# A fused embedding, attention and mixture-of-experts kernel: 16-bit turns, half-block turning moved, stores moved, last rows gathered elsewhere

## The reference

```python
h = tok(x)                                  # weight[x] + lora, times magnitude and a column norm
# attention: 16 heads of 32, every projection on quantised activations and weights
def act_quant(x):
    scale = 127 / clip(max(abs(x), -1), 1e-5)
    return clip(round(x * scale), -128, 127) / scale
bitlinear = lambda x, w: act_quant(x) @ weight_quant(w).T      # ternary weights
h = h + bitlinear(softmax(q k^T / sqrt(32)) v, w_o)            # q, k, v = bitlinear(layernorm(h), w)
# experts: a shared one of 704, and 2 of 8 routed ones of 352
g = softmax(x Wr^T); top 2
h = h + (silu(x Wsg^T) * (x Wsu^T)) Wsd + sum over the 2 of g_e * ((silu(x Wg_e^T) * (x Wu_e^T)) Wd_e)
```

## Time and profile before

| | us |
|---|---|
| median of 3 runs | 1512.48 |
| lowest, highest | 1511.66, 1517.18 |
| profiled execution | 1511.87 |
| its span in the trace | 1509.7 |

### The profile page before, as it was taken

One profiled execution on the slowest core, in us unless ns is written; L12 is line 12 of the kernel. 1 busy time (PEld: TensorE's weight loads), 2 busy tenths in 40 slices (PEclk: granted clock), 3 DMA queues, 4 the chain that ended last, 5 costly groups with the idle time before them and its releaser, 6 DMA issues.

```text
span 1509.7 us, 37446 instructions
## 1 busy us (share of the span) xinstructions
PE 1403.1 (93%) x14294; PEld 1146.5 (76%) x14294; DVE 1117.8 (74%) x2215; ACT 875.3 (58%) x1502; POOL 393.2 (26%) x494
## 2 busy tenths in 40 slices
PE   6587869999999996899999999999999999999997
PEld 1122147777777774899999998989889898999996
DVE  4477848889889885776647777877778777677776
ACT  4688936777777774433325666656556665533331
POOL 6500054444444420003211211111111110133333
PEclk9899979999999997899999999999999999999999
DMA  9999942223223111131114678777787776543365
GB/s 342 392 378 362 418 129 58 66 64 84 63 64 82 56 47 54 56 116 56 42 43 142 233 255 272 239 262 249 255 275 235 274 240 236 188 140 131 125 241 177
DMA packets 77905, 269.42 MB, mean 178 GB/s; under 512 B 9696, under 2 KB 10336, under 8 KB 71392
## 3 DMA queue, kind: packets, MB, share of 16 engines
q1 hardware_dynamic: 61360, 223.88, 41.0%
q0 software_dynamic: 16432, 44.05, 11.1%
HBM read 224.12 MB, written 43.78 MB: 177 GB/s over the span
## 4 chain that ended last, share of the span: by engine, by line
PE 33%; DVE 10%; issue 7%; ACT 7%; DMA 3%; POOL 0%; SPq 0%; ACTq 0%; POOLq 0%; DVEq 0%
PE up_ps L1734 6%; PE up_ps L1736 6%; PE up_ps L1735 6%; PE down_ps L1735 4%; PE down_ps L1736 4%; PE down_ps L1734 4%; DVE w_split L1509 3%; ACT w_split L1424 3%; DMA slot_rows<-y_rows 2%; DVE xT_lo L1500 2%; PE up_ps L1768 1%; DVE h L1645 1%; PE up_ps L1763 1%; DVE w_split L1510 1%; ACT h_hi L1446 1%
## 5 line engine op out<-in xcount | busy, mean ns | idle before, releaser
L1734 PE MATMUL up_ps<-xT_hi,w_split 128*128 128x256 f32 x1280 | 366.4, 286 | 15.6 <-DVE xT_lo L1500 8.3
L1736 PE MATMUL up_ps<-xT_hi,w_split 128*128 128x256 f32 x1280 | 362.8, 283 | 0.0
L1735 PE MATMUL up_ps<-xT_lo,w_split 128*128 128x256 f32 x1280 | 362.8, 283 | 0.0
L1734 PEld LDWEIGHTS up_ps<-xT_hi,w_split 128*128 128x128 f32 x1280 | 245.6, 192 | 18.6 <-issue 8.6
L1735 PEld LDWEIGHTS up_ps<-xT_lo,w_split 128*128 128x128 f32 x1280 | 245.7, 192 | 1.3
L1736 PEld LDWEIGHTS up_ps<-xT_hi,w_split 128*128 128x128 f32 x1280 | 245.6, 192 | 0.0
L1446 ACT ACTIVATE h_hi<-h 128x256 fp32r<-128x256 f32 (+1 forms) x192 | 80.2, 418 | 264.8 <-DVE h L1645 202.3
L1397 POOL DMA_INDIRECT xr<-x_rows,slot_tokens x71 | 71.5, 1006 | 426.1 <-PE xT_ps L1829 381.6
L1424 ACT ACTIVATE w_split<-w_stage 128x1408 fp32r<-128x1408 f32 (+1 forms) x123 | 169.1, 1411 | 4.4 <-PE down_ps L1736 1.8
L1734 PE MATMUL down_ps<-w_split,h_hi 128*128 128x512 f32 (+1 forms) x405 | 159.1, 393 | 1.4 <-DVE H L1629 1.4
L1736 PE MATMUL down_ps<-w_split,h_lo 128*128 128x512 f32 (+1 forms) x405 | 160.2, 396 | 0.0
(11 more groups left out here) (301 smaller groups left out, 3000.3 us busy)
## 6 DMA issues: line engine op xcount, KB each, us to landing
W<-table SPq DMA_DIRECT2D x48, 1280.0 KB, 8.7
w_stage<-packed SPq DMA_DIRECT2D x80, 704.0 KB
w_stage<-packed SPq DMA_DIRECT2D x40, 768.0 KB
xr<-x_turned SPq DMA_DIRECT2D x32, 512.0 KB
slot_rows<-y_rows SPq DMA_DIRECT2D x32, 512.0 KB
x_rows<-x SPq DMA_DIRECT2D x32, 256.0 KB, 2.0
x_turned<-x2T SPq DMA_DIRECT2D x32, 256.0 KB, 3.8
out<-H SPq DMA_DIRECT2D x32, 256.0 KB
```

Of the source, the lines that this page charges most:

```text
L1734: pe.matmul(out, a_hi, b_hi, start=first, stop=False)
L1735: pe.matmul(out, a_hi, b_lo, start=False, stop=False)
L1736: return pe.matmul(out, a_lo, b_hi, start=False, stop=last)
```

## The change

Four edits, as the diff has them. First, z and z2 are made with `ROUNDER + LOW_HALF`, LOW_HALF being 2^14, so that the low 16 bits of each f32 hold 16384 plus the integer. PE transposes only these 16-bit words, as bf16 with stride two and with the bf16 identity, into the first half of bank[3], and ACT reads them as int16, minus LOW_HALF. Second, the half block's h is turned into `route_ps`, after the first up part of the next block, and the wait for h_lo before up_ps[2] is gone. Third, SP issues the store of y ahead of the third weight piece. Fourth, the rows of the last two sequences are gathered into `xr[0]` and `xr[1]`, once the last block's rows have been read from them; sequences 28 to 31 are combined within the last block's body, 28 ahead of its last gate, and the last block's result is added to H last; SP's last four stores wait for that too.

```diff
...
 ROUNDER = 1.5 * 2.0**23
+LOW_HALF = 2.0**14
...
         bank = [ps(f"bank{i}", [P, 512]) for i in range(4)]
+        turned_words = bank[3][:, :].bitcast(mybir.dt.int16)[:, 0:D].rearrange("p (k t) -> p k t", k=KT)
...
                     act.wait_ge(quant2_done, back1.next)
-                    act.activation(z2[:, :], attn[:, :], ACT.Copy, bias=ROUNDER, scale=quant2[:, 0:1]).then_inc(z2_done, 1)
+                    act.activation(z2[:, :], attn[:, :], ACT.Copy, bias=ROUNDER + LOW_HALF, scale=quant2[:, 0:1]).then_inc(z2_done, 1)
...
                     act.wait_ge(aq_turned, back1.next)
-                    act.activation(aqT[:, :, :], bank[3][:, :].rearrange("p (k t) -> p k t", k=KT), ACT.Copy, bias=-ROUNDER).then_inc(aqT_done, 1)
+                    act.activation(aqT[:, :, :], turned_words, ACT.Copy, bias=-LOW_HALF).then_inc(aqT_done, 1)
...
                     after(act, xq_turned, ahead2.i - 1)
-                    act.activation(z[ahead2.b][:, :], y[ahead2.b][:, :], ACT.Copy, bias=ROUNDER, scale=quant[ahead2.b][:, 0:1]).then_inc(z_done, 1)
+                    act.activation(z[ahead2.b][:, :], y[ahead2.b][:, :], ACT.Copy, bias=ROUNDER + LOW_HALF, scale=quant[ahead2.b][:, 0:1]).then_inc(z_done, 1)
...
                     act.wait_ge(xq_turned, ahead2.next)
-                    act.activation(xqT[ahead2.b][:, :, :], bank[3][:, :].rearrange("p (k t) -> p k t", k=KT), ACT.Copy, bias=-ROUNDER).then_inc(xqT_done, 1)
+                    act.activation(xqT[ahead2.b][:, :, :], turned_words, ACT.Copy, bias=-LOW_HALF).then_inc(xqT_done, 1)
...
                 return mm
+            def turn_words(tile):
+                words = tile[:, :].bitcast(BF16)[:, 0::2]
+                for k in range(KT):
+                    mm = pe.transpose(bank[3][:, :].bitcast(BF16)[:, k * T:(k + 1) * T], words[:, k * P:(k + 1) * P], ident_b[:, :])
+                return mm
...
                         pe.wait_ge(xqT_done, now.next)
-                    turn(bank[3], z[ahead1.b]).then_inc(xq_turned, 1)
+                    turn_words(z[ahead1.b]).then_inc(xq_turned, 1)
...
                         pe.wait_ge(aqT_done, back2.next)
-                    turn(bank[3], z2).then_inc(aq_turned, 1)
+                    turn_words(z2).then_inc(aq_turned, 1)
...
             return 2 * no if ROUTED[r] == "B" else FULL_BLOCKS + no
+        def routed_tiles(odd):
+            return sum(2 if ROUTED[r] == "B" else 1 for r in range(odd, ROUTED_BLOCKS, 2))
...
             return "A" if n < B_FROM else ROUTED[n - B_FROM] if n < C_FROM else "C"
...
         def _(sp):
-            def load_weights(w, expert):
+            def load_weights(w, expert, before_last=None):
                 for piece, (a, b) in enumerate(PIECES):
+                    if piece == 2 and before_last is not None:
+                        store_rows(before_last)
...
                 sp.dma_start(xr[odd][:, :, :], x2T_dram[bass.ds((n - first) * 2, 2), :, :].rearrange("s p d -> p s d")).then_inc(rows_in[odd], 16)
-            def block_weights(r):
-                load_weights(r + 1, sp.value_load(block_expert[0:1, bass.ds(plan_no(r), 1)], min_val=0, max_val=EXPERTS - 1))
+            def block_weights(r, before_last=None):
+                load_weights(r + 1, sp.value_load(block_expert[0:1, bass.ds(plan_no(r), 1)], min_val=0, max_val=EXPERTS - 1), before_last)
...
             for r in range(ROUTED_BLOCKS - 3):
-                block_weights(r + 3)
-                store_rows(r)
+                block_weights(r + 3, r)
             load_rows(C_FROM, C_FROM % 2, C_FROM)
-            load_weights(LAST_W, EXPERTS + 1)
-            store_rows(ROUTED_BLOCKS - 3)
+            load_weights(LAST_W, EXPERTS + 1, ROUTED_BLOCKS - 3)
...
                 sp.dma_start(out[bass.ds(i, 1), :, :].rearrange("s p d -> (s p) d"), row(H, i)).then_inc(out_stored, 16)
-            with sp.Fori(0, SEQS) as i:
+            with sp.Fori(0, SEQS - 4) as i:
+                store_out(i)
+            for i in range(SEQS - 4, SEQS):
+                sp.wait_ge(y_taken, 2 * N - SEQS + i + 1)
...
             for i in range(SEQS):
-                after(pool, combined, (i - 1) * TOP)
+                if i < SEQS - 2:
+                    after(pool, combined, (i - 1) * TOP)
+                    rows, arrived = comb[i % 2], comb_in
+                else:
+                    pool.wait_ge(xT_lo_done, N)
+                    rows, arrived = xr[i % 2], rows_gathered
                 for t in range(TOP):
-                    pool.indirect_dma_start(out=comb[i % 2][:, t, :], out_offset=None, in_=y_dram,
-                                            in_offset=bass.IndirectOffsetOnAxis(ap=slot_i[:, t * SEQS + i:t * SEQS + i + 1], axis=0)).then_inc(comb_in[i % 2], 16)
+                    pool.indirect_dma_start(out=rows[:, t, :], out_offset=None, in_=y_dram,
+                                            in_offset=bass.IndirectOffsetOnAxis(ap=slot_i[:, t * SEQS + i:t * SEQS + i + 1], axis=0)).then_inc(arrived[i % 2], 16)
...
                 after(act, down_done, (n - 1) * 2)
-                act.activation(h_hi[odd][:, 0:2, 0:P], up_ps[2][:, 0:2 * P].rearrange("p (j t) -> p j t", j=2), ACT.Copy).then_inc(h_hi_done, 2)
-                act.activation(h_hi[odd][0:96, 2, 0:P], up_ps[2][0:96, 2 * P:3 * P], ACT.Copy).then_inc(h_hi_done, 1)
+                act.activation(h_hi[odd][:, 0:2, 0:P], route_ps[:, 0:2 * P].rearrange("p (j t) -> p j t", j=2), ACT.Copy).then_inc(h_hi_done, 2)
+                act.activation(h_hi[odd][0:96, 2, 0:P], route_ps[0:96, 2 * P:3 * P], ACT.Copy).then_inc(h_hi_done, 1)
...
                         dve.tensor_tensor(row(H, i), row(H, i), down_ps[r][:, :], ALU.add).then_inc(y_taken, 1)
-            def combine(i, odd):
-                dve.wait_ge(comb_in[odd], (i - odd) * TOP * 8 + TOP * 16)
+            def combine(i, odd, rows):
+                if rows is comb[odd]:
+                    dve.wait_ge(comb_in[odd], (i - odd) * TOP * 8 + TOP * 16)
+                else:
+                    dve.wait_ge(rows_gathered[odd], 16 * (TOP + routed_tiles(odd)))
...
                         dve.wait_ge(combined, i * TOP + t)
-                    dve.scalar_tensor_tensor(out=row(H, i), in0=comb[odd][:, t, :], scalar=gate_values[:, bass.ds(i, 1), t],
+                    dve.scalar_tensor_tensor(out=row(H, i), in0=rows[:, t, :], scalar=gate_values[:, bass.ds(i, 1), t],
                                              in1=row(H, i), op0=ALU.mult, op1=ALU.add).then_inc(combined, 1)
-            def gate_full(n, odd):
+            def gate_full(n, odd, before_last=None):
                 for j, (_, f) in enumerate(F_TILES):
+                    if before_last and j == 2:
+                        before_last()
...
                 for count, at, rows in ((2, 0, P), (3, 2, 96)):
-                    turned_h = up_ps[2][0:rows, at * P:count * P].rearrange("p (j t) -> p j t", j=count - at)
+                    turned_h = route_ps[0:rows, at * P:count * P].rearrange("p (j t) -> p j t", j=count - at)
...
                     gate_half_rows(n)
+                elif kind_after:
+                    gate_full(n, odd)
                 else:
-                    gate_full(n, odd)
+                    gate_full(n, odd, lambda: combine(SEQS - 4, 0, comb[0]))
+                    dve.wait_ge(combined, (SEQS - 3) * TOP)
...
                     dve.wait_ge(y_taken, n * 2)
-                    if not isinstance(n, int) or n > C_FROM + 1:
+                    if kind_after:
                         for r in range(2):
-                            combine((n - (C_FROM + 1)) * 2 + r, r)
+                            combine((n - (C_FROM + 1)) * 2 + r, r, comb[r])
+                    else:
+                        combine(SEQS - 3, 1, comb[1])
+                        combine(SEQS - 2, 0, xr[0])
+                        combine(SEQS - 1, 1, xr[1])
...
             each_block(dve, body, plan_blocks, plan_experts, plan_slots, mark_slots, None, read_table)
+            dve.wait_ge(combined, SEQS * TOP)
             take_y(N - 1, "C")
-            dve.wait_ge(y_taken, 2 * N)
-            for i in range(SEQS - 2, SEQS):
-                combine(i, i % 2)
...
                     mm.then_inc(up_done, 1)
+                    if j == 0 and kind_before == "H":
+                        turn_h(n - 1)
                 after(pe, h_done, (n - 1) * 4 + 3)
-                if kind_before == "H":
-                    pe.wait_ge(h_lo_done, n * 3)
...
                 for j, (start, f) in enumerate(F_TILES):
-                    mm = pe.transpose(up_ps[2][0:f, j * P:(j + 1) * P], rows[:, start:start + f], ident[:, :])
+                    mm = pe.transpose(route_ps[0:f, j * P:(j + 1) * P], rows[:, start:start + f], ident[:, :])
...
                     turn(n + 1, 1 - odd, kind_after)
-                if kind_before == "H":
-                    turn_h(n - 1)
...
```

## The result

| | before | after |
|---|---|---|
| median of the runs, us | 1512.07 (4 runs) | 1502.63 (4 runs) |
| lowest, highest | 1511.57, 1517.18 | 1501.38, 1505.97 |
| profiled execution | 1511.87 | 1505.97 |
| its span | 1509.7 | 1503.9 |

The ratio is 0.9934 [0.9919, 0.9949]: the change gives about 10 us. I forecast 1489 with 1484 to 1500, so the sign was right, the size was not: 9.4 of 23 us came. A second comparison, with a second profiled execution of the changed kernel (e14_after_again, span 1493.2), gave 0.9933 [0.9916, 0.995].

A forecast was written before the change was run, and what follows sets the result against it. The prediction took a chain mostly through PE to bound the kernel. From 1511.87 us it subtracted 6.1 (attention), 12.5 (half blocks) and 4.7 (tail), giving 1488.6, or 1489 for the median, with a range of 1484 to 1500.

The forecast's parts named there:

- What bounds the kernel: Whole kernel: a chain mostly through PE sets the end; PE's waits in attention, half blocks and DVE's tail are the places.
- Part 1: Attention: shorter 16-bit turns bring V's load 0.18 us earlier in 31 steps, plus 0.5 at the ends: 6.1 us.
- Rival A: Attention ring doesn't shorten because another input, likely DVE, ends last; gain 0.5 or nothing, 1495 us; chance 0.14.
- C: Attention: ACT's 16-bit read from PSUM costs double, 21 us worse than forecast, 1510 us, no change; chance 0.05.
- D: Attention: fewer busy PE columns let TensorE's clock fall, making the kernel slower, 1552 us with six such steps; chance 0.03.
- Parts 2 and 3: Half blocks: later turning of h and early store remove nearly all 13.0 us of PE waits: 12.5 us, bounds 8 and 13.8.
- the two weight pieces (first 1.41): Half blocks: ACT's splitting after h_hi, 1.4 us counted, within DVE's gate starting 8.4 us after PE's start, before 10.5.
- the ring: Half blocks: the loop through PE, ACT and DVE per five-block group becomes 59.8 us, level with PE's own 60.1.
- rival B: Half-block stall returns through late weights for ACT's first piece or longer DVE work, 1 us a group; 1495.5 us; chance 0.13.
- Part 4: Tail: early gathers and last block's sum last end DVE at 1502.3 instead of 1507.14; 4.7 us, bounds 3.2 and 5.4.
- The sum: Whole kernel: 1511.87 - 6.1 - 12.5 - 4.7 = 1488.6, with the median 0.6 higher 1489.2, say 1489; chance 0.65.

The follow-up runs named there:

- e14_after_again: The changed kernel run once more, unchanged, beside the others on the same chip; ratio 0.9933 to the kernel before.
- e5: The kernel before with only the turning of z and z2 as 16-bit words; ratio 0.9972.
- e6: e2 with the second weight piece loaded at half width in seven places, so partly wrong weights; ratio 0.9873 to the kernel before.
- e2: The changed kernel with only the store of the block ahead of each half block put behind the third weight piece again; ratio 0.9903 to the kernel before.
- e3: The changed kernel with its fourth edit, the tail, undone; ratio 0.9964 to the kernel before.
- e10: The changed kernel, all stores early, with the second weight piece at half width in seven places, so partly wrong weights; ratio 0.989 to the kernel before.
- e4: The changed kernel with unused matmuls added behind five half blocks (six each) and ahead of the last down matmuls (twelve); ratio 0.9926 to the kernel before.
- e9: e2 with 12 unused matmuls ahead of the last block's down matmuls; ratio 0.9898 to the kernel before.
- e11: e9 with row 28's sum moved behind the last gate; ratio 0.9887 to the kernel before.
- e12: The kernel of e2 once more, unchanged, beside later runs on the same chip; ratio 0.99 to the kernel before.

## Why the prediction was wrong

**What bounds the kernel** and the choice of places: right. The gain came from the three places named, in attention and in the tail by the mechanism given.

**Part 1, 6.1 us:** right, 5.1 and 6.2 us in the changed kernel's two traces, 6.1 in e5's. Rival A falls. A step of after, ACT and PE, against the earlier trace rows:

```profile
405.99 0.60 ACT L741 ACTIVATE xqT<-bank 128x512 bf16<-128x512 int16 x1
...
406.08 0.42 PEld L877 LDWEIGHTS bank<-ident,x 128*128 128x128 f32 x4 [0.31 <-ACT x L738]
...
406.70 0.63 PEld L959 LDWEIGHTS bank<-wT_v,xqT 128*128 128x128 bf16 x4
...
410.94 0.23 PEld L1029 LDWEIGHTS S<-maxT,pick 32*128 32x128 bf16 x16 [0.32 <-ACT maxT L708]
...
411.02 0.60 ACT L716 ACTIVATE aqT<-bank 128x512 bf16<-128x512 int16 x1
```

The copy starts as ACT's x ends (405.22 + 0.81 less the usual overlap of 0.04), with no idle time before it. The 16-bit read takes 0.60 us, as the f32 read did, so C falls. The wait for maxT grew from 0.17 to 0.32 (I said near 0.4). The 32 max transposes are at 232.5 to 577.6, 11.13 us a step against 11.27: 0.14 in a step, not 0.18, and 0.8 to 1.7 us at the end of the pipeline instead of 0.5. V's load did come 0.21 us closer behind x2's turn (0.62 us, where the earlier trace rows has 0.83), but V's four loads take 0.63 us instead of 0.56, and that takes 0.07 of it back. So the sum of 6.1 came out right with the step a little too large and the ends too small. The granted clock was 1.00 from 240 to 570: D falls.

**Parts 2 and 3, 12.5 us: the step that failed.** The order of events was right, and e6 shows it by number: gate 8.6 us after PE's start, groups of 60.4. ACT's y was no longer held by the store, and the waits of the earlier trace rows went. What failed is "the two weight pieces (first 1.41)": I took both as landed, because ACT waited only 4.4 us in all ahead of its splitting. But that row was made while PE's and ACT's own stall of 2 us hid the landing. The pieces' staging is freed by DVE's split of the earlier piece, so their DMA starts only in the half block, and the ring runs over DMA, ACT and DVE. In before, the issue of the second piece and the splitting of the first and second; then, from a DMA view of e2 (whose trace has the landings, before's has not) at the same place, KB and us from issue to landing:

```profile
1059.13 0.33 SPq L1306 DMA_DIRECT2D w_stage<-packed  x1
...
1064.69 2.65 ACT L1424 ACTIVATE w_split<-w_stage 128x1408 fp32r<-128x1408 f32 x2
```

```profile
w_stage<-packed SPq DMA_DIRECT2D x1, 704.0 KB, 7.4
```

ACT took the second piece at about 1066.0, 6.8 us after its issue. In my sum it takes it 3.4 + 0.4 + 1.4 = 5.2 us after PE's start, some 5.6 us after the issue. In e2 that piece lands 6.1 to 7.5 us after its issue in six of the seven places; in the first of the seven both pieces are issued over a microsecond sooner, and nothing waits. Shortening PE's wait shortened just the slack that this DMA had. And the change put a store into the same microseconds. DMA share and rate of after:

```profile
1054.00:1056.00 2.00, 0.67 (x4) 0.70 (x5) 2.00 (x6) 1.03 (x1) 1.70 (x2) 0.90 0.85 225
1056.00:1058.00 2.00, 2.00 (x11) 2.00 (x10) 1.53 (x2) 1.37 (x2) 0.72 (x1) 0.50 0.84 230
1058.00:1060.00 2.00, 2.00 (x15) 2.00 (x15) 1.38 (x2) 0.00 (x0) 0.00 (x0) 0.74 0.84 249
```

That is rival B with its "weights that land late", though B named ACT's first piece and it was the second. I gave it 0.13 and priced it at 1 us a group; it is 1.3 us a group with the early store (369.3, 367.5 and 368.3 us in after, e14 and e3, mean 368.4, against 6 x 60.1 = 360.6 forecast: 7.8 us) and 0.8 with one store behind (eight executions, mean 365.4). Of the 7.8, the second piece accounts for 5.9 (down to e10's 362.5), of which the store is 3.0 (down to 365.4). Of the rest, 1.9, about 1 us is that even a group in which nothing waits takes 60.2 to 60.3 us, not 60.1. For what then remains the likely cause is the third piece, for which e6 and e10 still show waits of 0.3 to 1.6 us on ACT; that was not tried by itself.

The clock is a small part of it. The same rows show 0.50 behind the wait of 2.21 us, and h is turned 4.36 us after PE's start instead of 2.88. In e14 waits of 2.19 and 2.22 us left it at 1.00:

```profile
1234.00:1236.00 2.00, 0.49 (x4) 0.52 (x5) 2.00 (x6) 0.50 (x1) 1.69 (x2) 1.00 0.95 291
1236.00:1238.00 2.00, 2.00 (x19) 2.00 (x19) 1.17 (x2) 1.91 (x2) 0.90 (x1) 1.00 0.98 259
```

With about the same waits in all (8.9 and 8.6 us) the stretches are 369.3, with two such drops, and 367.5, with none: at most 1.8 us.

**Part 4, 4.7 us:** the mechanism was right, one term mis-sized and one lacking. After again, DVE at the end, against the earlier trace rows:

```profile
1479.12 1.54 DVE L1664 SCALAR_TENSOR_TENSOR H<-comb,gate_values,H 128x512 f32<-128x512 f32 x2 [1.92 <-DMA comb<-slot_rows,slot_i]
1480.69 0.41 DVE L1678 TENSOR_TENSOR act_g<-act_g,up_ps 32x256 f32<-32x256 f32 x1
...
1489.44 1.28 DVE L1653 TENSOR_TENSOR H<-H,down_ps 128x512 f32<-128x512 f32 x2
```

DVE ends with both takes in a row and no gather waited for: the DVE-bound end that I forecast. The gate starts 3.17 us after PE's downs began instead of 1.8, so row 28's sum delays it by 1.4 us, not 0.6, for its gather lands 1.9 us after DVE is free. That makes 4.7 - 0.8 = 3.9, as measured. In the first execution of after PE was the bound instead:

```profile
1493.76 0.28 PEld L1770 LDWEIGHTS down_ps<-w_split,h_hi 128*128 128x128 f32 x1 [3.80 <-issue]
...
1498.15 0.69 DVE L1653 TENSOR_TENSOR H<-H,down_ps 128x512 f32<-128x512 f32 x1
1500.79 0.69 DVE L1653 TENSOR_TENSOR H<-H,down_ps 128x512 f32<-128x512 f32 x1 [1.95 <-PE down_ps L1772]
```

After a wait of 3.80 us in one piece the last downs ran at 0.50, and DVE waited 1.95 us for them. Before, PE's wait at this place was 1.84 us. I had not asked what it would grow to when the gate is put back, nor what PE's clock does behind it. The late silu is a second cost that no row of before shows.

**The sum.** 5.6 + 3.5 + 2.8 (means of the two executions) is 11.9 us against 23.3. The medians give 9.4, with 2.3 us either way by the interval of the ratio. 1502.6 is also about what I had priced A and B together at (1502), but that is chance: A didn't happen, B cost more than its price, and the tail lost 2 us for other reasons.

## What to carry to other kernels

- A row of little waiting on a transfer says nothing of the transfer's slack once the stall beside it is taken away. For each transfer in the shortened ring, take its issue time and its landing, and compare them with the new time of need. Here the issue and the use, 6.8 us apart, stood in the trace of before; the landing did not, and the sum left 5.6 us for it without asking.
- A store that is moved earlier moves into another transfer's time. One rule for all blocks (every store ahead) was worse than two (behind where a short block follows): 0.9934 and 0.9933 against 0.9903 and 0.99.
- Two short waits of an engine are not the same as one of their sum. Ask where a removed wait collects, and read the granted clock behind it.

## What the hardware showed that I had not expected

- TensorE's granted clock after waits of nearly the same length fell or stayed: 2.21 and 2.22 us with 0.50 behind them in after, 2.19 and 2.22 with 1.00 in e14; 3.80 with 0.50 in after, 3.50 with 1.00 in e14. With the 12 matmuls in the tail's gap (e4, e9, e11) it was 1.00 throughout.
- ACT's last third silu started 2.8 to 5.4 us after PE's last down stretch began in 7 of 12 executions of the changed tail, and 0.3 to 1.0 in the others, with the same code doing it or not (e2 on chip 2, e12 on chip 8). What it waited for is open, and so is whether it belongs to the gathers or to the chip.
- ACT reads 512 int16 values from PSUM in 0.60 us and turns them into bf16, the same as f32.
